# Cross-attention and quantized FFN on one core: the merge matrix split one score tile sooner, and batch 1's query turns moved one tile on

## The reference

```python
q      = layernorm(x)                               # rows of x, over D = 512
s      = einsum('bqd,bkd->bqk', q, ctx) / sqrt(512)
s      = where(mask, -1e9, s)
att    = softmax(s) @ ctx                           # keys and values are both ctx
x1     = x + einsum('bdl,ol->bdo', swapaxes(att), W_merge) + b_merge
z      = fake_quant(layernorm(x1))                  # one scale over the whole tensor
h      = fake_quant(silu(z @ Wg.T) * (z @ Wu.T))    # again one scale; Wg, Wu: 1408 x 512
out    = x1 + h @ Wd.T                              # Wd: 512 x 1408, weights fake-quantized by row
```

## Time and profile before

| what | value |
|---|---|
| median of 3 runs | 544.58 us |
| the profiled execution's own time | 543.5 us |
| its span | 541.7 us |
| TensorE busy | 528.9 us (98%) |
| VectorE busy | 436.7 us (81%) |
| ScalarE busy | 298.4 us (55%) |
| GpSimd busy | 150.1 us (28%) |

### The profile page before, as it was taken

The page is one execution under the profiler, slowest core; times in us unless marked ns, Lnnn a source line. Parts: engine busy times, 40 slices in busy tenths (PEclk is TensorE's granted clock), DMA queues, the critical chain, the costliest instruction groups (busy, mean ns, idle before and its releaser), DMA issues. The chain is left out here.

```text
span 541.7 us, 7377 instructions
## 1 busy us (share of the span) xinstructions
PE 528.9 (98%) x2468; PEld 346.6 (64%) x2468; DVE 436.7 (81%) x806; ACT 298.4 (55%) x446; POOL 150.1 (28%) x100
## 2 busy tenths in 40 slices
PE   7899999999999999999999999999999999999996
PEld 6777888888888888888887444444444444344442
DVE  5787999979799698896767587778878777699984
ACT  4775774757547575575240645554554543976610
POOL 3369455755457553674031000000000000000000
PEclk9999999999999999999999999999999999999999
DMA  8925579685875857843476539658301102779874
GB/s 271 302 63 133 179 180 160 230 191 176 200 126 205 201 170 194 140 157 90 119 62 185 220 47 326 219 169 276 106 10 39 39 1 71 298 291 390 271 252 155
DMA packets 77600, 93.61 MB, mean 173 GB/s; under 512 B 36096, under 2 KB 54528, under 8 KB 75008
## 3 DMA queue, kind: packets, MB, share of 16 engines
q1 hardware_dynamic: 77568, 93.21, 61.1%
HBM read 59.77 MB, written 25.43 MB: 157 GB/s over the span
## 5 line engine op out<-in xcount | busy, mean ns | idle before, releaser
L1292 PE MATMUL gu<-hid,gu_T 128*128 128x512 f16 x704 | 152.1, 379 | 0.0
L1292 PEld LDWEIGHTS gu<-hid,gu_T 128*128 128x128 f16 x704 | 68.8, 98 | 83.2 <-DVE hid L1202 0.4
L1100 ACT ACTIVATE hid<-gu,gu_mul 128x512 f32<-128x512 f32 x88 | 59.6, 685 | 73.5 <-PE gu L1292 68.0
L1183 DVE SCALAR_TENSOR_TENSOR hid<-gu,gu_mul,hid 128x512 f32 (+1 forms) x88 | 65.0, 746 | 32.4 <-PE gu L1292 28.4
L1335 PE MATMUL gu<-wd_T,gu_T 128*128 128x512 f16 x264 | 58.0, 379 | 1.1 <-DVE gu_T L1231 0.8
L834 PE MATMUL mm<-wm_hi,p_hi 128*128 128x512 f32 x128 | 52.5, 410 | 1.9 <-DVE wm_lo L552 1.9
L1191 DVE TENSOR_REDUCE hmax<-hid 128x1 f32 (+2 forms) x48 | 53.2, 1119 | 0.7 <-DVE hid L1183 0.7
L834 PE MATMUL mm<-cT_hi,qT_hi 128*128 128x512 f32 x128 | 50.5, 395 | 0.7 <-DVE cT_lo L546 0.7
L1129 ACT ACTIVATE h<-hid,inv 128x1024 int8<-128x1024 f32 (+3 forms) x31 | 43.5, 1479 | 13.4 <-DVE gu_T L1231 13.4
L836 PE MATMUL mm<-wm_hi,p_lo 128*128 128x512 f32 x128 | 50.2, 392 | 0.0
L835 PE MATMUL mm<-wm_lo,p_hi 128*128 128x512 f32 x128 | 50.0, 391 | 0.0
(11 more groups left out here) (142 smaller groups left out, 923.2 us busy)
## 6 DMA issues: line engine op xcount, KB each, us to landing
h_dram<-hid SPq DMA_DIRECT2D x3, 2816.0 KB, 9.3
hid<-h_dram SPq DMA_DIRECT2D x3, 2816.0 KB, 11.9
cb<-in_ctx_dram SPq DMA_DIRECT2D x28, 256.0 KB, 7.8
cx<-in_ctx_dram SPq DMA_DIRECT2D x7, 1024.0 KB, 10.3
x<-in_x_dram SPq DMA_DIRECT2D x5, 1024.0 KB, 5.7
x_dram<-x SPq DMA_DIRECT2D x20, 256.0 KB, 2.4
xq<-x_dram SPq DMA_DIRECT2D x5, 1024.0 KB, 10.4
x<-x_dram SPq DMA_DIRECT2D x5, 1024.0 KB, 4.8
```

The costliest lines, as they stand in the source:

```text
L1100: nc.scalar.activation(silu[SILU_AT[i]], gu[2 * (i % 3)][:], ACT.Silu, scale=gu_mul[:, 0, i:i + 1]).then_inc(silu_done, 1)
L1183: nc.vector.scalar_tensor_tensor(hid[:, b % SLOTS, i * L:(i + 1) * L], gu[2 * (i % 3) + 1][:], gu_mul[:, 1, i:i + 1], silu[SILU_AT[i]], AL ...
L1292: last = nc.tensor.matmul(gu[2 * (i % 3) + g][:], gu_T[:, g, h, i * P:(i + 1) * P], xT[p][:, h, :], start=h == 0, stop=h == T - 1)
```

## The change

The order of instructions changes in the streams of three engines. No computation is added or removed. On TensorE, W_merge's blocks 0 and 1 are turned behind score tile 0, block 2 behind tile 1, block 3 behind tile 2. The first two mixed tiles are done as row tiles 0 to 2 of tile 0, row tiles 0 to 2 of tile 1, then row tile 3 of each (`first_mixed`). Query turns of batch 1 stand behind mixed tile 2 (two of them) and mixed tile 3 (two), on ScalarE and VectorE as well. ScalarE and VectorE split W_merge's blocks sooner, and VectorE takes all of batch 1's row statistics behind the last score tile's maximum.

```diff
-                Q1_AFTER = ((), (0, 1), (2,), (3,))
+                Q1_AFTER = ((), (), (0, 1), (2, 3))
   # ScalarE, batch 0, for t in range(T):
                             exps(n, t)
                             if start:
+                                if t in (0, 2):
+                                    merge_hi(t + t // 2)
                                 if t < 2:
                                     transposed_hi(0, T + 2 + t)
                                 probs_hi(n, t)
-                                for k in ((0,), (1,), (2, 3), ())[t]:
-                                    merge_hi(k)
+                                if t < 2:
+                                    merge_hi(t + 1)
   # VectorE, batch 0, for t in range(T):
                             if start and t == T - 1:
+                                merge_lo(3)
                                 probs_lo(n, t - 1)
-                                merge_lo(2)
                             mask_and_max(n, t)
                             if start:
-                                if 0 < t < T - 1:
+                                if t == 0:
+                                    merge_lo(0)
+                                elif t < T - 1:
                                     probs_lo(n, t - 1)
-                                    merge_lo(t - 1)
-                                elif t:
-                                    merge_lo(3)
+                                    merge_lo(t)
+                                else:
+                                    row_stats1(1, 0, 1)
+                                invert_sum(n, t)
+                                if t == T - 1:
                                     row_stats1(1, 1, 2)
-                                invert_sum(n, t)
-                                if t == 2:
-                                    row_stats1(1, 0, 1)
-                                elif t == 3:
-                                    row_stats1(1, 2, 3)
                                 if t < 2:
                                     transposed_lo(0, T + 2 + t)
   # behind that loop
                             probs_lo(n, T - 1)
-                            row_stats1(n + 1, T - 1, T)
+                            row_stats1(n + 1, 2, T)
   # TensorE
+                    def first_mixed(k, rows):
+
+                        cols = slice(k * P, (k + 1) * P)
+                        for t in rows:
+                            pe.wait_ge(p_ready, t + 1)
+                            nc.tensor.matmul(mm[k][:], p_hi[:, t, cols], wm_hi[:, t, :], start=t == 0, stop=False)
+                            nc.tensor.matmul(mm[k][:], p_hi[:, t, cols], wm_lo[:, t, :], start=False, stop=False)
+                            last = nc.tensor.matmul(mm[k][:], p_lo[:, t, cols], wm_hi[:, t, :], start=False,
+                                                    stop=t == T - 1)
+                        if T - 1 in rows:
+                            last.then_inc(g_done, 1)
   # in mixed(n, k)
                             pe.wait_ge(x1_made, T * (n - 1) + k + 1)
-                        elif k == 0:
-                            pe.wait_ge(wm_ready, T)
   # behind scores(0, k)
-                                for g in ((0,), (1,), (2, 3), ())[k]:
+                                for g in ((0, 1), (2,), (3,), ())[k]:
                                     merge_transpose(g)
+                        if start:
+                            pe.wait_ge(wm_ready, T)
+                            for rows in (range(T - 1), range(T - 1, T)):
+                                for k in range(2):
+                                    first_mixed(k, rows)
                         for k in range(T):
                             if start:
-                                mixed(n, k)
+                                if k >= 2:
+                                    mixed(n, k)
                                 for g in Q1_AFTER[k]:
                                     transposes(n + 1, T + g)
```

## The result

The changed kernel takes 546.63 us (median of 15 runs) against 543.98 us for the kernel before (15 runs). The ratio is 1.0045, with a 95% interval of 1.0033 to 1.0058: slower by some 2.5 us. Both stood on the 544.58 us of three runs; the 15 runs put the kernel before 0.6 us lower. As a change, 1.0 us was forecast, the rival had 3.0 us, and the medians are 2.65 us apart.

A forecast was written before the change was run, and what follows sets the result against it. ScalarE's and VectorE's queues, 0.28 us behind TensorE, were taken to set batch 1's start, with VectorE's first maximum behind. 1.17 - 0.14 = 1.03 us net loss; 544.58 + 1.0 = 545.6 us, range 544.5 to 547.9 us.

The forecast's parts named there:

- the rival: Clock falls in TensorE's new gap before batch 1's scores, slowing score steps behind it; 547.6 us, chance 0.20.
- What held batch 1's start: Before batch 1's scores: TensorE's chain ends 0.28 us ahead of ScalarE's and VectorE's; scores start 1.17 us later, gap 4.15 us.
- the order of the two queues: On ScalarE and VectorE: one more mask and g_hi ahead of batch 1's first qT_hi, 1.00 us later.
- the moved statistics: On VectorE: two L578 behind the last p_lo instead of one; c_hi and all that hangs on it 0.15 us later.
- The splits, the row tiles and the statistics: Batch 0's mixed stage: wm_lo 3 ready in time, 2.0 us stall gone, mixed tiles without wait, statistics 0.15 us later.
- What is given back: At batch 1's first merged tile: the 0.14 us wait for the first maximum goes, leaving 1.03 us net.
- The second date, the first maximum: VectorE's first maximum of batch 1, at 51.70 us, lets the first merged tile start at 52.49 us at best.
- the chance of the clock: Lower clock behind the new gap doubles 6 to 18 score steps, costing 1.4 to 4.1 us, 2 taken; chance 0.20.
- The prediction's own sign of being wrong: Behind TensorE's gap before batch 1's scores: score steps lasting more than 0.23 us would show the forecast wrong.
- The rival of the other side: TensorE's lead before batch 1's scores is worth its size: up to 2.7 us gained, 541.9 us; chance 0.03.

The follow-up runs named there:

- e1: Changed kernel with ScalarE and VectorE taking batch 1's query turns in the order of before, TensorE as changed; ratio 1.0012 (0.9996 to 1.0027).
- e2: Kernel before with only the order of batch 1's query turns on ScalarE and VectorE changed; ratio 1.0012 (0.9997 to 1.0027).
- e5: Changed kernel with c_hi behind g_hi 1 on ScalarE and each query turn directly behind its g_hi on ScalarE and VectorE; ratio 1.0020.
- e3: Changed kernel with 11 extra 128x512 matmuls put into TensorE's gap before batch 1's scores; ratio 1.0016 (1.0004 to 1.0028).
- e9: e1 with 6 extra 128x512 matmuls put into TensorE's gap before batch 1's scores; ratio 1.0000 (0.9992 to 1.0009).
- e7: Kernel before with the ScalarE and VectorE edits of e5 and e6, without the change on TensorE or the earlier splits; ratio 1.0095.
- e11: Kernel before with the ScalarE and VectorE edits of e5 and e10, Q1_AFTER as it was; ratio 0.9990 (0.9975 to 1.0005).
- e10: e5 with the weights' cast behind batch 1's second maximum on VectorE and the clip factors in the last batch; 541.48 us, ratio 0.9945.
- e6: e5 with batch 1's maxima first on VectorE, the weights' cast behind batch 1's last p_lo, clip factors in the last batch; ratio 1.0101.
- e8: Changed kernel with only the clip factors moved to the last batch; ratio 1.0041 (1.0029 to 1.0054).
- e12: Changed kernel once more, unaltered, for a second trace; 548.49 us in one run.

## Why the prediction was right, and what it mis-sized

*What held batch 1's start* was right. TensorE was 0.28 us ahead of ScalarE's and VectorE's chain; its stall of 1.9 us went and that of 0.49 us shrank to 0.23 us, it was through 2.7 us sooner, and all of it stood as one gap before the scores. The delay was forecast as 1.17 us and is 1.18 us. Its parts are confirmed one by one: the order of the two queues 1.01 us (e1 against the changed kernel), 1.02 us (e2 against before); the moved statistics 0.15 us forecast, 0.17 us in e1.

*The splits, the row tiles and the statistics* went as worked out. `wm_lo` 3 ends in time (24.64 us against TensorE's 24.88), the first mixed tiles run without a wait, and `merge_hi(3)` found its place behind the exponential.

*What is given back* (0.14 us) fits too: e2 loses 0.86 us at the first merged tile after 1.02 us at the scores. The second date, the first maximum, is shown by e5, where 2.3 us gained at the scores gave no gain in the median.

*The step that failed is the chance of the clock.* It stood as a rival at 0.20, with a price of 1.4 to 4.1 us (2 taken), and the forecast of 1.0 us left it out. It happened in both traces of the changed kernel, and the mean clocks of all 15 runs fit it. Its price measures 3.65 - 2.05 = 1.6 us in the trace, within its bounds. The prediction's own sign of being wrong, score steps of more than 0.23 us behind the gap, came. Its reason against the fall, that TensorE's work is dense up to the gap and behind it, did not hold: the clock fell though it was dense. That no row bore the fall out was no evidence against it, since the trace of before has no gap of that length, and the slow transposes at the start were a sign that the lower level is where an idle array goes, though the granted clock reads 1.00 there.

1.18 + 1.6 - 0.14 = 2.64 us is the stage's 2.67 us. That the median moved by nearly the same, 2.65 us, is in part luck: the traced executions lie 1.1 us (changed) and 0.5 us (before) below their medians, and five of the 15 changed runs had more low clock than this fall. It was luck as well that a mechanism missing 1.6 us left the time only 1.0 us off: the three runs under the forecast had put the kernel before 0.6 us too high.

The Trainium skill (TensorE: Matmul & The Clock Gate, HAM oscillation) says that idle time between bursts brings the lower clock back; the traces with the gap (3.80, 3.83 us) agree, as do e3 and e9 without it. By the page the next burst starts cold; here it ran for some 1.0 us at the higher clock first. The falls behind 2.83 us (e1) and 1.84 us (e7, e11) come at shorter gaps than that section warns of. In both points the traces decide. Its Part 4 (PE-mode transpose) says that transposes don't count as activity in the same way. No run here varies the transposes alone, and it can't be the whole reason: e1 fell with eight transposes directly ahead of its gap, e7 and e11 with none there.

*The rival of the other side* (the lead is worth its size) was wrong for this change, for the reason given. e10 shows the other half: the lead is worth 2.4 us once three dates are met. The prediction named two of them, ScalarE's `c_hi` and VectorE's first maximum. It missed SyncE's wait for the cast, which e6 found the hard way.

## What to carry to other kernels

Before a stall is taken out, ask which date of another engine stands right behind it: here 0.28 us of slack decided, and 2 us of removed stall came back as idle time at the next meeting point. When a queue's order is moved along with TensorE's, check that the engine wasn't already the late one, since its order costs in full even while TensorE is early. And look at where small stalls are gathered into one: the same idle time in one piece can lower the clock, and it then costs more than its own length; filling it with spare matmuls is a cheap test. It is no full cure: it took the changed kernel from 1.0045 to 1.0016, still not below the kernel before.

## What the runs showed of the hardware that was not expected

**A short gap can be enough for the lower clock, but not every time.** It fell at gaps of 5.04 (e6), 4.14 (e5), 3.80 and 3.83 (the changed kernel), 3.83 (e8), 2.83 (e1) and 1.84 us (e7 and e11), and in the traces of before and e2 it did not behind 1.87 us. So of four stalls of nearly the same length, two brought the fall. In the traces of e2, e3 and e9 it didn't behind gaps of 1.0 to 1.2 us. In the changed kernel and in e1 the low stretch lasted some 3.4 us and cost about 1.5 us. Where other waits follow that take it up, it costs less: in e11 the scores start at 16.60 us, 0.7 us behind the 41.07 - 25.15 = 15.92 us at which TensorE was through in the trace of before. Of the 71 runs of the kernel before that stand beside the experiments, 30 have a mean granted clock of 0.997 or less, with a median of 544.20 us against 543.94 us for the others. So the kernel before seems to have such a fall in some executions at a small price, and the change takes that chance away in one place and brings a surer and dearer one in another; in which stretch those 30 runs were slow is not recorded.

**A tiny VectorE instruction can last 5 us.** The first clip-factor instruction (128x2, one addition) took 1.13 and 1.14 us in the two traces of the changed kernel, 1.27 us in that of before, and 5.00 us in e3, 4.98 us in e9 and 4.97 us in e5. In e3 VectorE's timeline and GpSimd's read:

```profile
47.73 5.00 DVE L688 TENSOR_SCALAR expc<-expc 128x2 f32<-128x2 f32 x1 [2.14 <-ACT expc L539]
```

```profile
47.65 5.06 POOL L374 TENSOR_TENSOR x<-x,bias 128x512 f32<-128x512 f32 x4
```

It ends at 52.73 us, when GpSimd's four additions end (52.71 us). The short case is a wait as well. VectorE's timeline of before, with its cast, and GpSimd's first addition:

```profile
46.95 1.27 DVE L686 TENSOR_SCALAR expc<-expc 128x2 f32<-128x2 f32 x1 [2.25 <-ACT expc L537]
...
48.46 1.01 DVE L690 TENSOR_SCALAR sig<-sig 128x2 f32<-128x2 f32 x1
49.39 2.39 DVE L681 CAST wst<-w 128x2048 f16<-128x2048 int8 x1
```

```profile
46.87 1.33 POOL L374 TENSOR_TENSOR x<-x,bias 128x512 f32<-128x512 f32 x1
```

The instruction ends at 48.22 us, when GpSimd's first addition ends (48.20 us). So it waits for one addition there and for all four in e3. In e3 nothing is left to wait for afterwards: the next such instruction (L692) takes 0.17 us in place of 1.01, and the cast 1.22 us in place of 2.39. From the start of the first clip-factor instruction to batch 1's first maximum it is 4.75 us before, 4.62 us in the changed kernel and 6.45 us in e3. The 5 us thus cost 1.7 to 1.8 us and not 4, and even the usual second date is in part GpSimd's doing. GpSimd gains where VectorE waits for all four: its additions take 5.06 us in e3, 6.02 us in e12 and 6.05 us in the trace of before.

The Trainium skill (GPSIMD Engine Reference, Key points) says that GpSimd shares its SBUF interfaces with VectorE and that they contend for some kinds of VectorE instructions; the rows are in line with that. Which of the two cases comes is open: GpSimd's first addition starts 0.06 to 0.12 us ahead of VectorE's instruction in the three long cases, and 0.08 to 0.19 us ahead in the short ones, so the order of the starts doesn't tell them apart. In e3 this put the first maximum at 54.18 us and left TensorE idle for 0.69 us before the first merged tile, in e9 for 1.67 us. The traces of e3, e5 and e9 are of executions 1.1 to 3.9 us above their medians. The kernel before has the same instruction in the same place, so a part of its own spread may come from it, which wasn't tested.
